# Small float32 products of an attention layer as float32r passes, and the order of the attention weights

## The reference, cut to what matters

```python
q, k, v = split(xt @ Wqkv + bqkv)          # q and k lose their mean over channels
k2n = k2 / (sum_c(k2) + 1e-7)              # k2 = k * k, per token
q2n = q2 / (sum_c(q2) + 1e-7)
k2n = k2n / max(norm_over_tokens(k2n), 1e-12)
q2n = q2n / max(norm_over_channels(q2n), 1e-12)
kv = k2n.T @ v                             # C x C
out = (v + q2n @ kv / sqrt(N)) @ Wln + bln
```

## Time and profile before

| | |
|---|---|
| device time, three runs | 1595.02, 1595.16, 1597.77 us (median 1595.16) |
| profiled execution | 1597.63 us, span 1596.0 us |
| mean granted TensorE clock | 0.968 of full speed |
| TensorE matmuls busy | 1459.9 us (91%), 9794 instructions |
| VectorE busy | 1361.9 us (85%), 2453 instructions |
| ScalarE busy | 1284.2 us (80%), 2568 instructions |
| GpSimd busy | 337.1 us (21%) |
| HBM | 29.29 MB read, 97.94 MB written, 80 GB/s |

### The profile page before, as it was taken

One profiled execution on the slowest core, in us unless ns is written; L12 is line 12 of the kernel. 1 busy time (PEld: TensorE's weight loads), 2 busy tenths in 40 slices (PEclk: granted clock), 3 DMA queues, 4 the chain that ended last, 5 costly groups with the idle time before them and its releaser, 6 DMA issues. The chain is left out here.

```text
span 1596.0 us, 28994 instructions
## 1 busy us (share of the span) xinstructions
PE 1459.9 (91%) x9794; PEld 1298.9 (81%) x9794; DVE 1361.9 (85%) x2453; ACT 1284.2 (80%) x2568; POOL 337.1 (21%) x232
## 2 busy tenths in 40 slices
PE   3439999999999999999999999999999999998983
PEld 2327888888888888889888888898888888988883
DVE  5678899989999898989998988999989899998436
ACT  2258888888889888888899888888998888877752
POOL 2321112221222122212221222222212222111000
PEclk8669999999999999999999999999999999999997
DMA  3010134434443444344433433444434334444431
GB/s 131 20 41 21 39 64 89 94 82 82 102 101 82 79 91 90 80 80 101 101 83 78 95 86 80 82 100 101 86 75 100 82 82 90 71 82 81 82 61 41
DMA packets 45576, 127.92 MB, mean 80 GB/s; under 512 B 3794, under 2 KB 4818, under 8 KB 45523
## 3 DMA queue, kind: packets, MB, share of 16 engines
q0 software_dynamic: 24480, 72.26, 27.8%
q1 hardware_dynamic: 20946, 54.98, 9.8%
q10 hardware_dynamic: 96, 0.00, 0.0%
HBM read 29.29 MB, written 97.94 MB: 80 GB/s over the span
## 5 line engine op out<-in xcount | busy, mean ns | idle before, releaser
L827 DVE SCALAR_TENSOR_TENSOR h<-xpad,dw_sb,h 128x784 f32<-128x784 f32 x512 | 503.1, 1050 | 0.0
L1369 POOL TENSOR_SCALAR xpad<-x,gn_rs 128x784 f32<-128x784 f32 x64 | 107.7, 1691 | 513.1 <-DVE x L886 498.1
L640 PE MATMUL tile_ps<-k,xT 112*128 112x256 f32 x896 | 200.8, 382 | 0.0
L1380 POOL TENSOR_TENSOR x_parts<-x,x_parts 128x784 fp32r<-128x784 f32 x64 | 117.1, 1849 | 358.9 <-ACT x_parts L1126 358.9
L640 PEld LDWEIGHTS tile_ps<-k,xT 112*128 112x128 f32 x896 | 171.2, 192 | 22.3
L566 PE MATMUL tile_ps<-wqk,xn_parts 128*112 128x256 f32 x1344 | 187.4, 294 | 0.0
L1066 ACT ACTIVATE junk<-x 128x784 bf16<-128x784 f32 x192 | 163.2, 857 | 24.3 <-DVE x L876 13.1
L1393 POOL DMA_DIRECT2D out<-row_sums x90 | 107.9, 1199 | 341.0 <-DMA out<-row_sums 215.4
L566 PEld LDWEIGHTS tile_ps<-wqk,xn_parts 128*112 128x112 f32 x1344 | 169.3, 175 | 0.1
L485 PE MATMUL conv_ps<-hq_parts,attn_parts 128*128 128x392 f32 x768 | 145.3, 344 | 23.4 <-DVE attn_parts L938 23.4
L485 PEld LDWEIGHTS conv_ps<-hq_parts,attn_parts 128*128 128x128 f32 x768 | 135.3, 188 | 33.1 <-DVE attn_parts L938 33.1
(11 more groups left out here) (154 smaller groups left out, 2825.2 us busy)
## 6 DMA issues: line engine op xcount, KB each, us to landing
out<-row_sums POOLq DMA_DIRECT2D x90, 784.0 KB, 7.1
x<-x SPq DMA_DIRECT2D x32, 784.0 KB, 4.3
out<-x SPq DMA_DIRECT2D x30, 784.0 KB, 3.4
expert_sb<-expert_rows SPq DMA_DIRECT2D x8, 256.0 KB, 4.9
out<-x SPq DMA_DIRECT2D x4, 392.0 KB, 2.3
x<-w_qk SPq DMA_DIRECT2D x1, 512.0 KB
x<-w_vT SPq DMA_DIRECT2D x1, 256.0 KB
x<-w_ln SPq DMA_DIRECT2D x1, 256.0 KB
```

What stands on the lines that cost most here:

```text
L640: mm = nc.tensor.matmul(tile_ps[:, KX_BANK, i * C:(i + 1) * C], xT[:, m, half(i)], k2[:, m, :], start=(m == 0), stop=(m == M - 1))
L827: nc.vector.scalar_tensor_tensor(acc, view, scalar, acc, ALU.mult, ALU.add).then_inc(dw_step[j].sem, 1)
L1369: nc.gpsimd.tensor_scalar(xpad[:, j, 1:1 + H, 1:1 + W], x1[:, B.odd, j, :].rearrange("p (h w) -> p h w", w=W), gn_r[:, 1, j:j + 1], gn_s[: ...
L1380: nc.gpsimd.tensor_tensor(x0_parts[:, 1, j, 0:HW], x0[:, Z.odd, j, :], x0_parts[:, 0, j, 0:HW].bitcast(F32), ALU.subtract).then_inc(x0_lo. ...
```

## The change

Rows that are equal within a strip are now used for more than their sum. Of the 32 equal rows of a strip, some carry the high part of the value and some the low part. In the first rows a tile written as float32r holds the value rounded; in the low rows a cut copy (the value times a mask column that is 1 there, rounded to float32r, and zero in the other rows) is subtracted first, so that they hold the rest. The product over all 128 rows then adds both with weights 1/16 (high) and 1/8 (low), in one float32r pass. `mix_const` carries the masks and weights. ScalarE's `key_rows` writes the cut into `attn_parts`, free at that time, and VectorE gets a new `key_rows`; `q_scales` gets two operations, `alpha_cut` and `alpha_rows`, in the free `kx_parts`. The key norms use two equal columns instead of one. Four operations are added to the setup.

The lists change too: attention weights come ahead of the gate's logits on TensorE and ahead of the sparsemax on VectorE; VectorE's key inverse stands between the halves of `q_low`, and the halves of `make_x3` follow each other; on ScalarE `normalise_x2` goes ahead of the key norm, the attention weights between the two `relu_h`, `x2_high` ahead of `normalise_x3`.

```diff
@@ TensorE
             def key_norms(E):
-                pe.wait_ge(ksum_read.sem, ksum_read.at(E))
+                pe.wait_ge(krow_ready.sem, krow_ready.at(E))
                 for c in range(J):
-                    mm = nc.tensor.matmul(tile_ps[:, KSUM_BANK, c:c + 1], k_rows[:, 1, half(c)], ones[:, 0:1], ...
+                    mm = nc.tensor.matmul(tile_ps[:, KSUM_BANK, 2 * c:2 * c + 2], k_rows[:, C + c * P:C + (c + 1) * P],
+                                          norm_weight[:], start=True, stop=True, skip_group_check=True)
@@ attention_weights
-                    nc.tensor.matmul(dst, k_rows[:, 0, half(c)], bv_ln[:], start=True, stop=False)
...
+                    mm = nc.tensor.matmul(dst, k_rows[:, half(c)], bv_ln[:], start=False, stop=True)
@@ query_scales
-                                              idn[:, row:row + 1].to_broadcast([P, P]), q_alpha[:, 1, :], start=True,
+                                              picks[:, strip:strip + 1].to_broadcast([P, P]), alpha_rows, start=True,
@@ TensorE step
                     key_norms(E)
+                    attention_weights(E)
                 if A.active:
                     gate_logits(A)
                 if E.active:
-                    attention_weights(E)
                     value_out(B, D, E, F, 1)
@@ VectorE
+            def key_rows(E):
+                dve.wait_ge(ksum_read.sem, ksum_read.at(E))
+                if (E - 1).active:
+                    dve.wait_ge(attn_w_mm.sem, attn_w_mm.at(E - 1))
+                nc.vector.tensor_tensor(k_rows[:], tile_ps[:, KSUM_BANK, :], k_cut.bitcast(F32),
+                                        ALU.subtract).then_inc(krow_ready.sem, 1)
@@ q_scales
                 nc.vector.reciprocal(q_alpha[:, 1, :], q_alpha[:, 0, :]).then_inc(alpha_step.sem, 1)
+                dve.wait_ge(alpha_step.sem, alpha_step.at(D, 2))
...
+                nc.vector.tensor_scalar(alpha_cut, q_alpha[:, 1, :], low_row, None, ALU.mult).then_inc(alpha_step.sem, 1)
+                dve.wait_ge(alpha_step.sem, alpha_step.at(D, 3))
+                nc.vector.tensor_tensor(alpha_rows, q_alpha[:, 1, :], alpha_cut.bitcast(F32),
+                                        ALU.subtract).then_inc(alpha_step.sem, 1)
@@ VectorE step
+                if E.active:
+                    key_rows(E)
                 if F.active:
                     box_scale(A, F)
                 if A.active:
                     gate_logits(A)
                 if E.active:
-                    q_low(E)
+                    q_low(E, 0)
                     key_norms(E)
+                    q_low(E, 1)
+                    attention_weights_low(E)
                 if A.active:
                     sparsemax(A)
                     mean_lows(A)
-                if E.active:
-                    attention_weights_low(E)
...
                 if E.active:
                     make_x3(E, 0)
+                    make_x3(E, 1)
                 if C_.active:
                     h_mask(C_)
-                if E.active:
-                    make_x3(E, 1)
@@ ScalarE
-                nc.scalar.copy(k_rows[:], tile_ps[:, KSUM_BANK, :].rearrange("p (a c) -> p a c", a=2)).then_inc(ksum_read.sem, 1)
+                nc.scalar.activation(k_cut, tile_ps[:, KSUM_BANK, :], ACT.Identity, scale=low_row).then_inc(ksum_read.sem, 1)
@@ ScalarE step
+                if D.active:
+                    normalise_x2(A, D)
                 if E.active:
                     key_norms(E)
-                if D.active:
-                    normalise_x2(A, D)
                 if C_.active:
                     relu_h(C_, 0)
-                    relu_h(C_, 1)
                 if E.active:
                     attention_weights_high(E)
+                if C_.active:
+                    relu_h(C_, 1)
+                if D.active:
+                    x2_high(D)
                 if F.active:
                     normalise_x3(F)
-                if D.active:
-                    x2_high(D)
```

More of the change, by code:

```diff
@@ L32 @@
 UNROLL = 2
+HIGH_ROWS, BIAS_LOW_ROWS = SUB // 2, SUB // 4
+PATTERNS = 4 + STRIPS
 STAGES = 7
@@ L133, in build @@
         expert_sb = sb("expert_sb", [P, PACKED, STRIPS, J * C])
-        mix_const = sb("mix_const", [P, EXPERTS + SUB])
+        mix_const = sb("mix_const", [P, EXPERTS + SUB + PATTERNS])
+        low_row, bias_low_row, bias_weight, norm_row, pick_rows = (
+            mix_const[:, EXPERTS + SUB + a:EXPERTS + SUB + b] for a, b in ((0, 1), (1, 2), (2, 3), (3, 4), (4, PATTERNS)))
+        norm_weight = sb("norm_weight", [P, 2], F32R)
+        picks = sb("picks", [P, STRIPS], F32R)
         dw_sb = sb("dw_sb", [P, J, TAPS])
@@ L223, in build @@
         k_inv = sb("k_inv", [P, 2, J])
-        k_rows = sb("k_rows", [P, 2, C])
+        k_rows = sb("k_rows", [P, 2 * C], F32R)
+        k_cut = attn_parts[:, 0].rearrange("p j c -> p (j c)")
+        alpha_cut, alpha_rows = kx_parts[:, 0, 0, 0:QUARTER], kx_parts[:, 1, 0, 0:QUARTER]
         conv_ps = ctx.enter_context(nc.psum_tensor("conv_ps", [P, 4, 512], F32))
@@ L527, in attention_weights @@
                 pe.wait_ge(kx_lo.sem, kx_lo.at(E))
-                pe.wait_ge(ksum_read.sem, ksum_read.at(E))
+                pe.wait_ge(krow_ready.sem, krow_ready.at(E))
                 for c in range(J):
                     dst = tile_ps[:, ATTN_BANK, c * C:(c + 1) * C]
-                    nc.tensor.matmul(dst, k_rows[:, 0, half(c)], bv_ln[:], start=True, stop=False)
                     for i in range(J):
                         for u, v in ((0, 0), (0, 1), (1, 0)):
-                            mm = nc.tensor.matmul(dst, kx_parts[:, u, i, half(c)], w_out[:, v, i, :], start=False,
-                                                  stop=(i == J - 1 and u == 1))
+                            nc.tensor.matmul(dst, kx_parts[:, u, i, half(c)], w_out[:, v, i, :],
+                                             start=(i == 0 and u == v), stop=False)
+                    mm = nc.tensor.matmul(dst, k_rows[:, half(c)], bv_ln[:], start=False, stop=True)
                 mm.then_inc(attn_w_mm.sem, 1)
@@ L920, in box_row_sums, with q_low @@
                 nc.vector.tensor_tensor(*row_operands(1), ALU.add).then_inc(row_step.sem, 1)
[L922 to L926, removed]
+            def q_low(E, j):
+                dve.wait_ge(q_hi.sem, q_hi.at(E, j + 1))
+                nc.vector.tensor_tensor(q_parts[:, 1, j, :], q2[:, j, :], q_parts[:, 0, j, :].bitcast(F32),
+                                        ALU.subtract).then_inc(q_lo.sem, 1)
+            def key_rows(E):
[4 more added lines that the diff above has]
+                                        ALU.subtract).then_inc(krow_ready.sem, 1)
             def key_norms(E):
@@ L1152, in key_rows @@
                 act.wait_ge(ksum_mm.sem, ksum_mm.at(E))
-                nc.scalar.copy(k_rows[:], tile_ps[:, KSUM_BANK, :].rearrange("p (a c) -> p a c", a=2)).then_inc(ksum_read.sem, 1)
+                nc.scalar.activation(k_cut, tile_ps[:, KSUM_BANK, :], ACT.Identity, scale=low_row).then_inc(ksum_read.sem, 1)
             def key_norms(E):
                 act.wait_ge(knorm_mm.sem, knorm_mm.at(E))
-                nc.scalar.activation(k_norm[:], tile_ps[:, KSUM_BANK, 0:J], ACT.Sqrt, scale=1.0 / SUB).then_inc(knorm_read.sem, 1)
+                sums = tile_ps[:, KSUM_BANK, 0:2 * J].rearrange("p (c k) -> p c k", k=2)[:, :, 0]
+                nc.scalar.activation(k_norm[:], sums, ACT.Sqrt).then_inc(knorm_read.sem, 1)
             def fourth_powers(D):
@@ L1411 @@
 SETUP_BN = SETUP_PARTS + 2
[L1412 removed]
+SETUP_DVE = SETUP_BN + 10 + 2 + 2 + 2 + 3 + 4
 SETUP_CENTRED = 12 + 6
@@ L1429 @@
     group_mean = ((c[:, None] // GROUP) == (c[None, :] // GROUP)).astype(np.float32) / (GROUP * HW)
+    row, strip = c % SUB, c // SUB
+    low, bias_low = row >= SUB - BIAS_LOW_ROWS, (row >= HIGH_ROWS) & (row < SUB - BIAS_LOW_ROWS)
+    picked = (strip[:, None] == np.arange(STRIPS)[None, :]) & ((row == 0) | (row == SUB - 1))[:, None]
     per_channel = {
@@ L1441 @@
         "mix_pattern": np.concatenate([c[:, None] // SUB == np.arange(EXPERTS)[None, :] % STRIPS,
-                                       c[:, None] % SUB == np.arange(SUB)[None, :]], axis=1).astype(np.float32),
+                                       c[:, None] % SUB == np.arange(SUB)[None, :],
+                                       low[:, None], bias_low[:, None], np.where(low | bias_low, 1.0 / BIAS_LOW_ROWS,
+                                                                                 1.0 / HIGH_ROWS)[:, None],
+                                       np.where(low, 1.0 / BIAS_LOW_ROWS, np.where(bias_low, 0.0, 1.0 / HIGH_ROWS))[:, None],
+                                       picked], axis=1).astype(np.float32),
         "dw_w": L1_conv_dw_w,
```

20 lines of the change are left out of this document (13 added, 7 removed).

## The result

The changed kernel takes 1556.52 us (median of four runs, 1556.38 to 1557.04) against 1595.38 (now four runs of the kernel before); the ratio is 0.975, 95% interval 0.9735 to 0.9765. The profiled execution took 1556.38 us with a span of 1554.7, 41 us under that of before, whose profiled execution was 2 us above its median.

The account below looks back on a forecast made before the run. VectorE was to bind in TensorE's place: 43.6 work + 1.0 waits + 0.1 port = 44.7 us a step, 21.6 less over 28 steps, 7.8 less in the tail, 1.4 more setup: 1567 us, range 1548 to 1590 (own range 1556 to 1578).

Parts of the forecast that it names:

- The bound changes engine: One step: TensorE falls from 44.7 to 42.8 us, VectorE's work rises from 42.4 to 43.6 and binds.
- Prices: TensorE's single passes shed 1.88 us a step (bias 0.73, norms 0.18, scales 0.97); VectorE's additions cost 1.18.
- Rival D: Query scales on TensorE: float32r at 196 columns gains nothing, only the tail loses; 1571 us; forecast including it 0.56.
- The waits: VectorE's waits in a step fall from 3.0 to 1.0 us; the 1.68 at x2_low and TensorE's 0.78 go.
- Part 3: Timeline of one step in the new order: VectorE reaches x2_low 8.5 us after the group-mean copy, finding it ready.
- A: VectorE's waits go in full except the root's 0.28; a step saves 1.57 us; 1545 us, chance 0.12.
- B: Half the waiting returns, ScalarE 0.5 late in two places; step 45.3 to 45.5, 1587 us, chance 0.17.
- C: Slower: key_rows delays TensorE's key norms, x2_low's 1.68 wait stays whole; step 46.6, 1622 us, chance 0.07.
- TensorE's wait in front of the norms: Sign of being right: TensorE waits once a step, about 1.5 to 2 us, for VectorE's key_rows.
- VectorE's old work: VectorE's own work in a step of the kernel before, 42.4 us, carried over with the additions on top.
- The port: VectorE's row sums collide with GpSimd's x1 pass: 0.1 us a step; in full 0.64, 1582 us, chance 0.08.
- Outside the 28 steps: Last four images and setup: 7.8 us less in the tail, 1.4 more for four added setup operations.

Follow-up runs that it names:

- the order alone: Kernel before with the new order of all three engine lists and none of the new arithmetic; 1569.33 us, ratio 0.982.
- the tuned run: Kernel after, reordered further: key_rows in the variances' root wait, gate operations earlier, h_mask between row sums, ScalarE's squares of x0 later; 1585.33 us, ratio 0.9909.
- The two tuned runs: The tuned run (1585.33 us), and the same with ScalarE's x0 high part moved ahead of x0's squares (1552.12 us, ratio 0.971).

## Why the prediction was right

**The bound changes engine.** Right. I had put the step at 44.7, it is 44.08; 0.8 us of VectorE work more lengthens it by 0.8 (and brings the clock down besides). VectorE binds together with 0.9 us of waits, nearly all for ScalarE, and filling the largest of them gained nothing. What I had too simple is the kernel before: TensorE was busy for 44.7 of 45.47 us, but with 1.75 us taken from it and the old order kept, the step stayed. No run lightens TensorE without loading VectorE, so the two can't be separated further.

**Prices.** The added VectorE work was 1.18 by my sum, 0.61 + 0.64 = 1.25 in the trace. TensorE was to shed 1.88; by the rows it shed 0.12 at the norms, 0.73 at the bias and 0.90 at the scales, 1.75. The four records at the scales take 0.43, where I had 0.36. Rival D is out: 196 columns do gain.

**The waits.** `x2_low`'s and TensorE's waits went as worked out, attention's low part kept 0.42 (I had 0.5), and the wait at the second mask was filled. A new one of 0.20 stands at `h_mask`; it came with the new order, for the order alone has it too (0.24) while it still waits at the second mask. In all 0.89 against my 1.0. Even the moments of Part 3 hold: `x2_low` starts 785.27 - 776.86 = 8.4 us behind the step's start, where I had 8.5. The rivals A, B and C are out by these rows. TensorE's wait in front of the norms is 1.09 in the mean, under the 1.5 to 2 that I had given as a sign, since the step came out shorter and TensorE's work a little longer.

**The term that was mis-sized** is VectorE's old work, which I carried over at 42.4 unchanged. The depthwise taps took 441.3 us over the 28 steps before and take 430.8 now: (441.3 - 430.8)/28 = 0.38 less a step, because GpSimd's `x0_low` is released earlier and ends by the time at which the last five taps begin. The first of the five taps on VectorE and the second pass of `x0_low` on GpSimd, in the kernel before and then in the kernel after:

```profile
834.55 1.36 DVE L827 SCALAR_TENSOR_TENSOR h<-xpad,dw_sb,h 128x784 f32<-128x784 f32 x1
```

```profile
833.52 1.57 POOL L1380 TENSOR_TENSOR x_parts<-x,x_parts 128x784 fp32r<-128x784 f32 x1
```

```profile
771.53 1.03 DVE L841 SCALAR_TENSOR_TENSOR h<-xpad,dw_sb,h 128x784 f32<-128x784 f32 x1
```

```profile
769.83 1.57 POOL L1411 TENSOR_TENSOR x_parts<-x,x_parts 128x784 fp32r<-128x784 f32 x1
```

Before, the tap started 0.54 us ahead of the pass's end (835.09) and ended 0.82 behind it, as in the tuned run; after, the pass is over at 771.40 and the tap is short. The two tuned runs show the size of that: 4.86 or 6.06 us for the same five. The Trainium skill's page "SBUF — State Buffer", section "Who interferes with whom", gives the rule (a VectorE instruction with two SBUF inputs against a GpSimd instruction that reads SBUF; the lock is exclusive). The trace agrees, with 6.06 against 4.86, and with a tap that ended 0.8 us behind the end of GpSimd's pass in both cases. I had looked for it in one place only, the row sums. With 0.38, and 0.1 each for the waits and for the port, which took nothing from the row sums' total, less 0.07 for the dearer additions, the 44.7 becomes 44.2; the last 0.1 is spread over small operations.

**The port.** The first row sum (`L918`, now `L932`) did become longer, and the second (`L920`, now `L934`) shorter by as much: the collision moved from the second pass to the first, and the sum stayed at 4.2. The 0.1 that I had put down for it was not lost. That the collision can be avoided altogether (both at 1.79, in the run that fills the 0.42 wait) I had not considered.

**Outside the 28 steps** I had 7.8 less and 1.4 more, and got 4.1 less and 1.7 more. So the steps gave 38.9 where the forecast had 21.6, and the rest gave 2.4 where it had 6.4. The two misses partly cancel, and the time stands at the low end of the forecast's own 1556 to 1578: that it lies inside is in part luck.

What the prediction did not see is that the second group of passes is a loss: 8 us with the query scales, 6 with the keys, medians of different rounds (6 to 7 for each by the ratios). My own numbers held it, TensorE at 42.8 and VectorE at 43.6.

## What to carry to other kernels

Where the busiest engine has a neighbour a few per cent behind, lay out one step with all waits: work moved from the first to the second pays only until they are level, here after one of two groups. Look at durations as well as waits: here two engines that hold each other up show it in five operations that take 6.1 us instead of 4.7, and in no wait. A wait that is filled comes back downstream if another chain of the same step is as long.

## What the runs showed of the hardware

With TensorE waiting 1.9 us in each step, its granted clock fell to 0.50 for 3.4 us behind the wait in eight of 28 steps, and each of these was 1.7 us longer; eight products nobody reads, put into that wait, kept the clock at 1.00 and saved 10.5 us in all. Shorter waits, 0.86 and 0.16 us close together, were followed by the same in seven of 28 steps of another run, while those of the kernel after, one a step and up to 1.27, never were. And a VectorE operation on two columns took 0.52 us instead of 0.17 with GpSimd's pass over x1 beside it.
